# First three batches with the adapter as the stationary side, and x of the second batch sent by ScalarE's queue

## What is computed

```python
y = einsum('bij,bkj->bik', x, weight[adapter_ids])            # 8 batches, 128 x 512, adapter 512 x 512
q = y[:, 107:127, :].mean(axis=1)
routing = softmax(q @ router_W.T + router_b)                  # 8 experts
base = y @ W.T + b
t = einsum('bsd,erd->bser', y, A)                             # rank 16 each
out = x + base + einsum('bser,eor,be->bso', t, B, routing) * 2.0
```

## Time and profile before

| | |
|---|---|
| median of 3 runs | 71.73 us (71.39 to 71.83) |
| profiled execution, its own time | 72.28 us |
| span of its instructions | 70.6 us |
| TensorE busy (matmuls) | 65.2 us, 92% |
| VectorE busy | 42.0 us, 59% |
| ScalarE busy | 30.4 us, 43% |
| read from HBM, written | 12.08 MB, 2.10 MB |
| granted clock of TensorE | full in all 40 slices |

### The profile page before, as it was taken

The page is one execution under the profiler, slowest core; times in us unless marked ns, Lnnn a source line. Parts: engine busy times, 40 slices in busy tenths (PEclk is TensorE's granted clock), DMA queues, the critical chain, the costliest instruction groups (busy, mean ns, idle before and its releaser), DMA issues.

```text
span 70.6 us, 1064 instructions
## 1 busy us (share of the span) xinstructions
PE 65.2 (92%) x374; PEld 52.2 (74%) x374; DVE 42.0 (59%) x98; ACT 30.4 (43%) x62; POOL 1.2 (2%) x10
## 2 busy tenths in 40 slices
PE   2996987999999999999999999999999999999940
PEld 1331423755699998998998988889999988889920
DVE  1000020748989999949999999994293245138230
ACT  0800032857698996658763693300330444000000
POOL 5100000000000000000000000000000000000000
PEclk9999999999999999999999999999999999999999
DMA  0459899999999999999734204224633000004922
GB/s 0 134 194 393 285 395 388 408 406 412 418 409 409 409 409 406 409 409 411 307 153 102 47 0 104 54 44 110 154 149 149 0 0 0 9 0 134 312 74 74
DMA packets 7590, 15.30 MB, mean 217 GB/s; under 512 B 800, under 2 KB 4000, under 8 KB 7584
## 3 DMA queue, kind: packets, MB, share of 16 engines
q1 hardware_dynamic: 6720, 14.64, 55.6%
q10 hardware_dynamic: 864, 0.59, 3.2%
HBM read 12.08 MB, written 2.10 MB: 201 GB/s over the span
## 4 chain that ended last, share of the span: by engine, by line
PE 80%; DMA 9%; SPq 5%; issue 1%; DVE 0%; DVEq 0%
PE ps_o L594 30%; DMA wc_raw<-in_wcT_dram 9%; PE ps_t L594 8%; PE ps_o L622 8%; PE ps_y L555 5%; PE ps_y L577 4%; PE ps_y L579 4%; PE ps_y L578 4%; SPq L199 3%; PE ps_o L555 3%; PE ps_yT L577 3%; PE ps_yT L578 3%; PE ps_yT L579 3%; PE ps_yT L588 3%; PE ps_y L594 2%; SPq L204 1%
## 5 line engine op out<-in xcount | busy, mean ns | idle before, releaser
L594 PE MATMUL ps_o<-yT_hi,az_hi 128*128 128x256 f32 (+1 forms) x52 | 15.7, 301 | 0.0
L594 PE MATMUL ps_o<-yT_lo,az_hi 128*128 128x256 f32 (+1 forms) x52 | 15.4, 297 | 0.0
L594 PE MATMUL ps_o<-yT_hi,az_lo 128*128 128x256 f32 (+1 forms) x52 | 15.4, 296 | 0.0
L404 DVE TENSOR_TENSOR wc_lo<-wc_raw,wc_hi 128x1024 fp32r<-128x1024 f32 x10 | 11.9, 1215 | 0.1
L594 PEld LDWEIGHTS ps_o<-yT_hi,az_hi 128*128 128x128 f32 x52 | 9.8, 188 | 0.4
L594 PEld LDWEIGHTS ps_o<-yT_hi,az_lo 128*128 128x128 f32 x52 | 9.8, 188 | 0.5
L594 PEld LDWEIGHTS ps_o<-yT_lo,az_hi 128*128 128x128 f32 x52 | 9.8, 188 | 0.3
L309 ACT CAST wc_hi<-wc_raw 128x1024 fp32r<-128x1024 f32 x10 | 10.0, 1050 | 0.0
L476 DVE SCALAR_TENSOR_TENSOR wc_raw<-ps_o,rest_raw,xT_raw 128x256 f32<-128x256 f32 (+1 forms) x12 | 6.2, 542 | 6.0 <-PE ps_o L622 6.0
L555 PE MATMUL ps_y<-wc_raw,xT_raw 128*128 128x512 f32 x16 | 7.4, 597 | 0.5 <-DMA wc_raw<-in_wcT_dram 0.5
L642 PE MATMUL ps_l<-warm 128*128 128x512 bf16 x11 | 4.8, 625 | 1.3 <-DVE warm L481 1.3
(11 more groups left out here) (84 smaller groups left out, 114.6 us busy)
## 6 DMA issues: line engine op xcount, KB each, us to landing
wc_raw<-in_wcT_dram SPq DMA_DIRECT2D x16, 512.0 KB, 12.3
rest_raw<-in_rest_dram SPq DMA_DIRECT2D x2, 512.0 KB, 9.7
xT_raw<-in_xT_dram SPq DMA_DIRECT2D x2, 512.0 KB, 14.3
out_dram<-wc_raw SPq DMA_DIRECT2D x2, 512.0 KB, 3.1
xT_raw<-in_xT_dram SPq DMA_DIRECT2D x3, 256.0 KB, 7.1
yT_raw<-y_turn SPq DMA_DIRECT2D x12, 64.0 KB, 2.1
out_dram<-wc_raw SPq DMA_DIRECT2D x3, 256.0 KB, 2.3
rest_raw<-in_rest_dram SPq DMA_DIRECT2D x1, 278.0 KB, 8.1
```

The lines of the kernel that those rows point to most:

```text
L404: tt(flat(wc_lo[b % 2][:, part_h, :]), flat(wc_raw[:, b, part_h, :]), flat(wc_hi[b % 2][:, part_h, :]).bitcast(F32), ALU.subtract).then_in ...
L594: last = mm(bank, stat[:, n, c, :], yT[mov][:, c].rearrange("p b s -> p (b s)"), start=(start and c == 0 and k == 0), stop=(stop and c == ...
```

## The change

The first three batches swap the roles of the operands: the adapter's 128 x 128 blocks are the stationary side, and x (128 columns) moves. y then comes out with features on the partitions, so these batches need no copy and no transposes. Each of them takes 16 products of 128 columns in place of 4 of 512. The split half of batch 1 goes, and with it ScalarE's and VectorE's work for it and four semaphores. Batches 0 and 2 use the bank `ps_y`, batch 1 `ps_yT`, and ScalarE rounds straight from there.

The order on TensorE becomes: batches 0 and 1, half of batch 2, `project_t(0)`, `logits(0)`, the other half of batch 2, `base(0, 0)`. x of batch 1 is no longer in SyncE's queue: ScalarE sends it after waiting for adapter 0's first half. ScalarE's order becomes `hi_yT(0)`, `hi_yT(1)`, `hi_az(0)`, `hi_x(3)`, `hi_az(1)`. The interleaved order of features is given up: batch 3's copy is plain, the host no longer applies `turned`, and VectorE's `turn` (batches 4 to 7) reads PSUM with four elements between neighbours instead.

```diff
+        def yT_bank(b):
+            return ps_yT if b % 2 else ps_y
+
...
+        def load_x_alone(queue, b):
+            queue.dma_start(flat(xT_raw[:, b]), xT0[b]).then_inc(x_arrived(b), 16)
+
...
             load_wc(0, 0)
             load_wc(0, 1)
-            load_x(1)
             load_wc(1, 0)
...
-            def copy_y(b, bank):
-                act.wait_ge(y_done, b + 1)
-                copy(y_sb.rearrange("p (c t k) -> p c t k", c=C, k=NT),
-                     bank[:].rearrange("p (c k t) -> p c t k", c=C, k=NT)).then_inc(y_copied, 1)
+            def copy_y(b):
+                act.wait_ge(y_done, b - RAW + 1)
+                copy(y_sb[:], y_bank(b)[:]).then_inc(y_copied, 1)
...
-                    copy(yT_home(yT_hi, yT4_hi, b), per_chunk(ps_yT[:])).then_inc(yT_hi_ready, 1)
+                    copy(yT_home(yT_hi, yT4_hi, b), per_chunk(yT_bank(b)[:])).then_inc(yT_hi_ready, 1)
...
-            act.dma_start(flat(xT_raw[:, 0]), xT0[0]).then_inc(x_arrived(0), 16)
+            load_x_alone(act, 0)
             act.wait_ge(warm_ready, 1)
             nc.scalar.activation(junk[:], warm[:, 0:1], ACT.Exp)
 
-            hi_x1()
-            copy_y(0, ps_y)
-            for c in range(HALF, C):
-                hi_wc1(c)
+            act.wait_ge(wc_in[0][0], 16)
+            load_x_alone(act, 1)
+
             hi_yT(0)
-            copy_y(1, ps_o[3])
+            hi_yT(1)
             hi_az(0)
-            hi_yT(1)
             hi_x(3)
             hi_az(1)
-            copy_y(2, ps_y)
             hi_az(2)
...
             def turn(b):
-                dve.wait_ge(y_done, b + 1)
+                dve.wait_ge(y_done, b - RAW + 1)
                 nc.vector.transpose(y_turn[b % 2].rearrange("p k c s -> p c k s"), y_bank(b)[:].rearrange(
-                    "p (c k s) -> p c k s", c=C, k=NT)).then_inc(y_turned, 1)
+                    "p (c s k) -> p c k s", c=C, k=NT)).then_inc(y_turned, 1)
...
-            lo_x1()
-            for c in range(HALF, C):
-                lo_wc1(c)
             lo_yT(0)
             lo_az(0)
             lo_yT(1)
...
-            def y_raw(b, c, bank):
+            def y_across(b, c):
                 if c == 0:
                     pe.wait_ge(x_arrived(b), 16)
+                    if b >= 2:
+                        pe.wait_ge(q_ready, b - 1)
                 if c % HALF == 0:
                     pe.wait_ge(wc_in[b][c // HALF], 16)
-                last = mm(bank[:], xT_raw[:, b, c, :], wc_raw[:, b, c, :], start=(c == 0), stop=(c == C - 1))
+                for o in range(C):
+                    last = mm(yT_bank(b)[:, o * S:(o + 1) * S], wc_raw[:, b, c, o * P:(o + 1) * P], xT_raw[:, b, c, :],
+                              start=(c == 0 and o == 0), stop=(c == C - 1 and o == C - 1))
                 if c == C - 1:
-                    last.then_inc(y_done, 1)
...
+                    last.then_inc(yT_done, 1)
...
-            for c in range(C):
-                y_raw(0, c, ps_y)
+            for b in range(2):
+                for c in range(C):
+                    y_across(b, c)
             for c in range(HALF):
-                y_raw(1, c, ps_o[3])
-            pe.wait_ge(ident_ready, 1)
-            transpose_y(0)
-            for c in range(HALF, C):
-                y1_split(c, ps_o[3])
-            for c in range(C):
-                y_raw(2, c, ps_y)
-                if c == 0:
-                    transpose_y(1)
+                y_across(2, c)
+            pe.wait_ge(az_lo_ready, 1)
+            project_t(0)
             pe.wait_ge(ones_ready, 1)
             logits(0)
-            pe.wait_ge(az_lo_ready, 1)
-            project_t(0)
+            for c in range(HALF, C):
+                y_across(2, c)
             pe.wait_ge(az_lo_ready, 2)
             base(0, 0)
-            transpose_y(2)
```

More of the change, by code:

```diff
@@ L127, in adapter_lora_kernel @@
         wc_lo_ready = sem("wc_lo_ready")
[L128 to L131, removed]
         y_done = sem("y_done")
@@ L208, in load_x @@
             def load_x(b):
-                sp.dma_start(flat(xT_raw[:, b]), xT0[b]).then_inc(x_arrived(b), 16)
+                load_x_alone(sp, b)
             def load_x_pair(g):
@@ L310, in hi_wc @@
                         .then_inc(wc_hi_ready, 1)
[L312 to L318, removed]
             def exponent(g):
@@ L358, in _ @@
             hi_wc(4)
-            copy_y(3, ps_y)
+            copy_y(3)
             hi_x(5)
@@ L362, in _ @@
             hi_wc(5)
-            act.wait_ge(y_done, 5)
+            act.wait_ge(y_done, 5 - RAW)
             hi_x(6)
@@ L368, in _ @@
             hi_yT(4)
-            act.wait_ge(y_done, 6)
+            act.wait_ge(y_done, 6 - RAW)
             hi_x(7)
@@ L405, in lo_wc @@
                        flat(wc_hi[b % 2][:, part_h, :]).bitcast(F32), ALU.subtract).then_inc(wc_lo_ready, 1)
[L407 to L415, removed]
             def lo_yT(b):
@@ L421, in lo_yT @@
                 if b < ON_PE:
-                    tt(lo, per_chunk(ps_yT[:]), hi.bitcast(F32), ALU.subtract).then_inc(yT_lo_ready, 1)
-                    nc.vector.tensor_reduce(sums, per_chunk(ps_yT[:])[:, :, Q_START:Q_END], AX.X, ALU.add)\
+                    tt(lo, per_chunk(yT_bank(b)[:]), hi.bitcast(F32), ALU.subtract).then_inc(yT_lo_ready, 1)
+                    nc.vector.tensor_reduce(sums, per_chunk(yT_bank(b)[:])[:, :, Q_START:Q_END], AX.X, ALU.add)\
                         .then_inc(q_ready, 1)
@@ L548, in _ @@
             mm = nc.tensor.matmul
-            def y_raw(b, c, bank):
+            def y_across(b, c):
                 if c == 0:
                     pe.wait_ge(x_arrived(b), 16)
+                    if b >= 2:
+                        pe.wait_ge(q_ready, b - 1)
                 if c % HALF == 0:
                     pe.wait_ge(wc_in[b][c // HALF], 16)
-                last = mm(bank[:], xT_raw[:, b, c, :], wc_raw[:, b, c, :], start=(c == 0), stop=(c == C - 1))
+                for o in range(C):
+                    last = mm(yT_bank(b)[:, o * S:(o + 1) * S], wc_raw[:, b, c, o * P:(o + 1) * P], xT_raw[:, b, c, :],
+                              start=(c == 0 and o == 0), stop=(c == C - 1 and o == C - 1))
                 if c == C - 1:
-                    last.then_inc(y_done, 1)
-            def y1_split(c, bank):
-                if c == HALF:
-                    pe.wait_ge(x1_lo_ready, 1)
-                pe.wait_ge(wc1_hi_ready, c - HALF + 1)
-                mm(bank[:], xT_hi[1][:, c, :], wc_hi[1][:, c, :], start=False, stop=False)
-                mm(bank[:], xT_lo[1][:, c, :], wc_hi[1][:, c, :], start=False, stop=False)
-                pe.wait_ge(wc1_lo_ready, c - HALF + 1)
-                last = mm(bank[:], xT_hi[1][:, c, :], wc_lo[1][:, c, :], start=False, stop=(c == C - 1))
-                if c == C - 1:
-                    last.then_inc(y_done, 1)
+                    last.then_inc(yT_done, 1)
             def y_split(b, c):
@@ L572, in y_split @@
                 if c == 0:
+                    if b == RAW:
+                        pe.wait_ge(q_ready, b)
                     pe.wait_ge(xT_lo_ready, b - RAW + 1)
@@ L583, in transpose_y @@
             def transpose_y(b):
-                pe.wait_ge(y_copied, b + 1)
-                if b > 0:
-                    pe.wait_ge(q_ready, b)
+                pe.wait_ge(y_copied, b - RAW + 1)
+                pe.wait_ge(q_ready, b)
                 for c in range(C):
@@ L674, in _ @@
             base(0, 3)
+            pe.wait_ge(ident_ready, 1)
             transpose_y(3)
@@ L729, in contraction_first @@
         return np.ascontiguousarray(m)
-    def turned(m):
-        axis = m.ndim - 3
-        m = m.reshape(*m.shape[:axis], 4, 32, *m.shape[axis + 1:])
-        return np.ascontiguousarray(np.swapaxes(m, axis, axis + 1)).reshape(*m.shape[:axis], P, *m.shape[axis + 2:])
     az = np.concatenate([a.reshape(e * r, d), w]).reshape(c + 1, P, d)
-    consts = np.concatenate([turned(contraction_first(rw)).reshape(P, c * e), np.broadcast_to(rb.reshape(1, e), (P, e)),
+    consts = np.concatenate([contraction_first(rw).reshape(P, c * e), np.broadcast_to(rb.reshape(1, e), (P, e)),
                              bias.reshape(c, P).T], axis=1)
     xT = contraction_first(x).reshape(nb, P, c, s)
-    azT = turned(contraction_first(az)).reshape(c + 1, P, d)
+    azT = contraction_first(az).reshape(c + 1, P, d)
     bT = b.transpose(0, 2, 1).reshape(e * r, d)
```

## The result

The changed kernel takes 74.95 us in the median of six runs (73.93 to 76.5) against 71.83 (71.39 to 72.98) for the kernel before. The ratio is 1.0411, with a 95% interval of 1.0363 to 1.046. I had forecast 71.6, no measurable change. The profiled execution of the changed kernel took 74.96 us at a span of 73.2. Some executions of either kernel take 1 to 3 us longer, in part with a stretch of TensorE at its lower clock; the ratios given here leave them out, and where a median of few runs holds them I give the lowest run beside it.

A forecast was written before the change was run, and what follows sets the result against it. The prediction took the second batch's start plus TensorE's work after it as the bound. +0.10 us for work and wait and -0.25 for an earlier start gave -0.15: 71.73 becomes 71.6 us, range 70.9 to 72.9.

The forecast's parts named there:

- What bounds the kernel: Whole kernel: time is the second batch's start (11.05 us), TensorE's work after it, and a 2.8 us tail.
- The price of a product: TensorE, adapter stationary: 0.1095 us a record, two records a product, 3.50 us a batch.
- Rival (a): TensorE's new products: weight loads don't hide behind 128 columns, 0.16 us a record, 74.9 us; chance 0.10.
- TensorE's work and the new wait: After the second batch's start: 0.90 us less work, 0.90 us wait ahead of the projection, 0.1 restart; net +0.10 us.
- The start of the second batch: Loads of x and the second adapter: TensorE starts 0.25 us earlier, between 0.55 earlier and 0.3 later.
- rival (b): Second batch's x on ScalarE's queue lands late, at 11.5 to 12.3 us, behind 0.5 to 1 MB more; 72.8 us; chance 0.12.
- The smaller edits: Removed copies, split and semaphores, and VectorE's strided transposes: taken as nothing; upper end costs 0.8 us.
- The chances: Whole kernel: within 1% 0.66, faster by over 1% 0.12, slower by over 1% 0.22.
- (d): VectorE's strided transposes cost its strided sum's rate, or records take 0.118 us: +0.3 to +0.8, 72.2 us; chance 0.13.

The follow-up runs named there:

- Experiment 1: Changed kernel with x of the second batch back in SyncE's queue and nothing else sent by ScalarE; 71.98 us, ratio 1.0041 to the kernel before.
- experiment 3: Changed kernel with ScalarE sending x of the second batch directly behind x of the first; 73.44 us median of four runs, lowest 72.51.
- experiment 6: Changed kernel with SyncE waiting for adapter 0's first half before asking for adapter 1; 72.34 us, ratio 1.0097.
- experiment 8: Experiment 1 with three third-batch chunks ahead of the projection, and VectorE making the second batch's low part before the A chunk's; 71.66 us, ratio 0.9995.
- experiment 2: Kernel before with only x of the second batch moved to ScalarE's queue, after adapter 0's first half; 75.64 us median of four runs, lowest 73.96.
- experiment 10: Changed kernel with SyncE waiting for adapter 0's first half after asking for both halves of adapter 1; 76.07 us median of four, lowest 74.69.

## Why the prediction was wrong, step by step

**What bounds the kernel** held: the start of the second batch plus TensorE's work. After the LoRA product nothing moved (-0.09 us).

**The price of a product** held nearly: 0.112 us a record against 0.1095 taken and 0.107 to 0.118 as bounds. On 64 records that is +0.15 us. Rival (a), loads that don't hide, fell, and with it the estimate of 0.155 us by the ratio of the Trainium skill (TensorE: Matmul & The Clock Gate, section "Back-to-back issue gap").

**TensorE's work and the new wait** held: -0.90 and +0.90 + 0.10 were forecast, a wait of 0.82 us came, and the stretch to the LoRA product grew by 0.24 where I said 0.10. The 0.15 of the records is not the whole of that difference: the second batch's first step was 0.1 us longer and not the 0.24 that I had added, and from the second batch's last result (17.35 us) to the projection (19.95) it took 2.60 us and not 2.50. Experiment 1, which has this and not the queue, is +0.2 us by medians, +0.3 by the ratio.

**The start of the second batch** is the step that failed. I wrote that x "lands at 9.2 us at the earliest, and near 10 with shared engines", and took 0.25 us of gain with 0.3 us of loss as the worst end. It landed at 13.46. The row on which it stood was the 2.7 us of a load on idle engines, and it says nothing about a loaded queue; the range of this term should have reached to the other transfers of SyncE's queue in the profile of before (KB, median us to landing):

```profile
wc_raw<-in_wcT_dram SPq DMA_DIRECT2D x16, 512.0 KB, 12.3
xT_raw<-in_xT_dram SPq DMA_DIRECT2D x3, 256.0 KB, 7.1
```

A transfer issued at 6.7 us with the same 7.1 us lands at 13.8, and that was there to read. The mechanism is rival (b), to which I gave 0.12 and "0.5 to 1 MB more", and its sign came: x landed last, after both halves of its adapter (10.1 and 11.4 us). The trace has 1.3 MB in front of x, and then 3.3 us for 256 KB in shared running. So (b) was also under-priced, at 72.8. The rule of the Trainium skill that I set beside it (DMA: Bandwidth & Descriptors, section "Queues, rings and completion order"), round-robin by packet, did not put x ahead of what was already asked for: 3.5 us passed before x's first packet. The landing near 10 us that I read out of it was wrong by 3.5 us.

**The smaller edits** held: VectorE's transposes 708 against 706 ns, and nothing of the removed casts and copies shows in experiment 1.

**The chances**: the slow side got 0.22 and happened. Its carriers were (a) at 0.10, refuted, (b), which had 0.12, and a part of (d), refuted too. That the measured 74.95 us is (a)'s price of 74.9 is chance: its records of 0.16 us were 0.112.

## What to carry to other kernels

A load that waits for an event and then goes out on a second queue does not overtake all that the other queue has asked for: here 1.3 MB went ahead of its first packet, and three times its own size beside it. Before moving a load to a later moment, count the bytes asked for by then, and keep it in the position that its consumer needs. Here x came early from the second queue only when it was asked for first (experiment 3) or when the other queue was held (experiment 6), and neither was faster than x left in SyncE's queue (experiment 1). And where a chain through other engines comes behind a product, place as much TensorE work between as the chain lasts, but look at the next chain too (here the logits'), since the wait moves there.

## What I had not expected of the hardware

- The same instructions find TensorE at 1.2 or 2.4 GHz from one execution to the next. Up to the first product the kernels of experiments 1 and 8 are the same on TensorE, and the first batch took 5.55 us in the one profile and 3.81 in the other.
- The clock fell to the lower level during a wait of about 3 us in one execution of experiment 2 and came back some 7 us later; in the profiled execution of experiment 10, with a wait of 2.5 us, it did not fall.
- With one adapter half loaded as two transfers, in pieces of half the length, the DMA engines moved 285 in place of 350 GB/s at the same busy share. It cost 0.6 us against experiment 8 and 1.1 against the kernel before, although TensorE could start 0.7 us earlier.
